# Router stage of a mixture-of-experts layer: its four batches written out and pipelined, per-chunk loads, a scan for the running counts

## The reference

```python
x = hidden_states.reshape(-1, h)
logits = jnp.einsum('th,eh->te', x, router_w)
top_vals, top_idx = jax.lax.top_k(logits, TOP_K)
top_w = jax.nn.softmax(top_vals, axis=-1)
expert = top_idx[:, 0]
weight = top_w[:, 0]
...
combine = jax.nn.one_hot(expert, e, dtype=x.dtype) * weight[:, None]
out = jnp.einsum('eth,te->th', out_e, combine)
```

```python
base = jax.nn.sigmoid(r.astype(jnp.float32)) * (num / jnp.maximum(den, 1e-08))
out = base * (0.8 + 0.2 * tf)
```

## Time and profile before

| what | value |
|---|---|
| median of 3 runs | 2638.8 us (2637.32 to 2645.15) |
| the profiled execution's own time | 2640.12 us |
| its span, first to last instruction | 2638.4 us |
| busy in the span | PE 81%, PEld 50%, DVE 67%, ACT 51%, POOL 41% |
| mean granted TensorE clock | 0.903 |

### The profile page before, as it was taken

One profiled execution on the slowest core, in us unless ns is written; L12 is line 12 of the kernel. 1 busy time (PEld: TensorE's weight loads), 2 busy tenths in 40 slices (PEclk: granted clock), 3 DMA queues, 4 the chain that ended last, 5 costly groups with the idle time before them and its releaser, 6 DMA issues. The chain is left out here.

```text
span 2638.4 us, 43862 instructions
## 1 busy us (share of the span) xinstructions
PE 2124.7 (81%) x14585; PEld 1320.6 (50%) x14585; DVE 1771.3 (67%) x3464; ACT 1349.1 (51%) x3201; POOL 1092.5 (41%) x748
## 2 busy tenths in 40 slices
PE   0688887999999999999954499727887887875899
PEld 0355554656555566666634355414555555542344
DVE  7788877888878887867643299545767677753110
ACT  4566655555555555555534133235656565635432
POOL 5656565555545565544420255443323233320000
PEclk9989998999999999999985599957888888887999
DMA  4233223211222122211125744462333232326110
GB/s 157 76 96 97 85 87 98 97 65 58 70 89 84 65 74 66 93 61 62 63 86 219 283 136 136 165 246 77 120 105 120 90 136 81 105 92 223 72 72 24
DMA packets 114027, 279.00 MB, mean 106 GB/s; under 512 B 10576, under 2 KB 40656, under 8 KB 111184
## 3 DMA queue, kind: packets, MB, share of 16 engines
q1 hardware_dynamic: 94032, 221.69, 24.8%
q10 hardware_dynamic: 17280, 46.93, 5.0%
q0 software_dynamic: 2560, 8.39, 0.8%
HBM read 188.89 MB, written 80.74 MB: 102 GB/s over the span
## 5 line engine op out<-in xcount | busy, mean ns | idle before, releaser
L828 PE MATMUL ps_q<-a_y,a_w 128*128 128x512 f16 x1536 | 355.4, 381 | 0.0
L614 POOL TENSOR_TENSOR a_rb<-a_rb,a_rot 128x512 f32<-128x512 f32 x129 | 185.9, 1441 | 308.1 <-ACT a_rb L727 308.1
L828 PEld LDWEIGHTS ps_q<-a_y,a_w 128*128 128x128 f16 x1536 | 149.3, 101 | 162.7 <-issue 4.0
L182 POOL TENSOR_TENSOR wkv_ekv<-wkv_ek,wkv_kt 128x512 f32<-128x512 f32 x66 | 100.9, 1529 | 308.6 <-DVE wkv_ek L215 308.6
L255 DVE TENSOR_TENSOR_SCAN wkv_bwd<-wk_decay,wkv_tail,wkv_fwd 128x512 f32<-128x512 f32 x130 | 215.1, 1684 | 0.7
L618 POOL TENSOR_TENSOR a_qk<-a_ra,a_rb 128x512 f32<-128x512 f32 x129 | 204.6, 1586 | 18.9 <-POOL a_rb L614 0.5
L878 PE MATMUL ps_g<-a_o,a_wo 128*128 (+1 forms) x768 | 176.3, 379 | 13.2 <-POOL a_o L605 10.6
L845 PE MATMUL ps_s<-a_qk 128*128 128x512 f32 (+3 forms) x512 | 174.1, 462 | 14.3 <-POOL a_qk L618 14.3
L837 PEld LDWEIGHTS ps_v<-a_w,a_y 128*128 128x128 f16 x3072 | 176.9, 98 | 15.1
L867 PE MATMUL ps_o<-a_tt_,a_v 128*128 128x512 f32 (+3 forms) x512 | 174.2, 487 | 11.0 <-ACT a_tt_ L745 9.4
L837 PE MATMUL ps_v<-a_w,a_y 128*128 128x128 f16 x3072 | 182.0, 219 | 0.0
(11 more groups left out here) (249 smaller groups left out, 4876.3 us busy)
## 6 DMA issues: line engine op xcount, KB each, us to landing
a_w<-wqkv_split SPq DMA_DIRECT2D x48, 768.0 KB, 4.3
scratch_numlog<-wkv_nl ACTq DMA_DIRECT2D x48, 512.0 KB, 2.8
wkv_kt<-in_fT ACTq DMA_DIRECT2D x67, 256.0 KB, 2.7
a_wraw<-in_wqkv SPq DMA_DIRECT2D x18, 768.0 KB, 5.5
wqkv_split<-a_w SPq DMA_DIRECT2D x17, 768.0 KB, 7.1
a_stacks<-qk_parts SPq DMA_DIRECT2D x102, 128.0 KB, 2.6
gate_up<-in_gate_up SPq DMA_DIRECT2D x8, 1408.0 KB, 23.5
a_nlc<-scratch_numlog SPq DMA_DIRECT2D x18, 512.0 KB, 4.1
```

The source lines that it names most:

```text
L614: pool.tensor_tensor(rb[:, n, :], rb[:, n, :], rot[:, 2 * n + 1, :], ALU.mult).then_inc(s["roped"], 1)
L828: mm = pe.matmul(psq[n][:], w16[:, i % 2, wp, n, c, :], y16[:, yp, c, :], start=c + m == 0, stop=c == CC - 1 and m == 2)
```

## The change

What it does, all of it in `moe_route`:

- The loops over the batches are written out. `mr_xt` has two buffers, y is written in place in them, and `mr_yt` is gone. Batch b uses buffer b % 2.
- SP issues x of batches 0 and 1 without a wait, x of batch b >= 2 once the transposes of batch b-2 are done (`rows_ps`). The division's terms come in four DMAs of 512 KB, one for each chunk, each of which waits for that chunk's y of the batch before. ACT's first exp waits for x alone; DVE waits for its chunk's terms.
- The copies of a batch's rows on ACT, and of its logits on DVE (with the 8 largest of its four tiles, which were all taken at the end), stand behind the next batch's elementwise work. PE has two banks for logits and four for rows.
- The 16 dependent additions become one scan over 128 columns, expert-major, with a factor of 0 where an expert's row begins (`going`, made by POOL). The counts now include the tile itself, so the constant matrix `prior` changes from 1 and 0 to 0 and -1. The memset of the first count is gone.

```diff
-        xt = sb("xt", [P, CC, T])
+        xt = sb("xt", [P, 2, CC, T])
         nl = sb("nl", [P, CC, 2, T])
-        yt = sb("yt", [P, CC, T])
...
                 for b in range(B):
-                    if b:
-                        sp.wait_ge(s["sig"], b * CC)
-                    sp.dma_start(xt[:], d["x1"][b].rearrange("c p n -> p c n")).then_inc(s["x_loaded"], 16)
-                    if b:
-                        sp.wait_ge(s["y"], b * CC)
-                    sp.dma_start(nl[:], d["numlog"][1, b].rearrange("c p m n -> p c m n")).then_inc(s["x_loaded"], 16)
+                    if b >= 2:
+                        sp.wait_ge(s["rows_ps"], (b - 1) * TT)
+                    sp.dma_start(xt[:, b % 2], d["x1"][b].rearrange("c p n -> p c n")).then_inc(x_loaded[b % 2], 16)
+                    for c in range(CC):
+                        if b:
+                            sp.wait_ge(s["y"], (b - 1) * CC + c + 1)
+                        sp.dma_start(nl[:, c], d["numlog"][1, b, c]).then_inc(nl_loaded[c], 16)
                 for e in range(E):
                     sp.dma_start(w.gate_up[:, e], d["gate_up"][:, e]).then_inc(w.loaded[e], 16)
                     sp.dma_start(w.down[:, e], d["down"][:, e]).then_inc(w.loaded[e], 16)
...
-                with act.Fori(0, B) as b:
-                    act.wait_ge(s["x_loaded"], b * 32 + 32)
+                for b in range(B):
+                    y = xt[:, b % 2]
+                    act.wait_ge(x_loaded[b % 2], b // 2 * 16 + 16)
...
-                    for t in range(TT):
-                        act.wait_ge(s["rows_ps"], b * TT + t + 1)
-                        act.activation(rows[:, bass.ds(b * TT + t, 1), :].rearrange("p a n -> p (a n)"),
-                                       pst[t % 2][:], ACT.Copy).then_inc(s["rows"], 1)
+                    if b:
+                        take_rows(b - 1)
+                take_rows(B - 1)
...
-                with pe.Fori(0, B) as b:
+                for b in range(B):
+                    y = xt[:, b % 2]
                     pe.wait_ge(s["y"], b * CC + CC)
+                    if b >= 2:
+                        pe.wait_ge(s["logits"], b - 1)
...
                     for t in range(TT):
-                        if t >= 2:
-                            pe.wait_ge(s["rows"], b * TT + t - 1)
+                        if b:
+                            pe.wait_ge(s["rows"], (b - 1) * TT + t + 1)
...
-                then(dve.memset(before[:, 0, :], 0.0))
...
-                for i in range(NT):
-                    then(dve.tensor_tensor(before[:, i + 1, :], before[:, i, :], onehot[:, i, :], ALU.add))
+                then(dve.tensor_tensor_scan(upto.rearrange("p e t -> p (e t)"), going[:].rearrange("p e t -> p (e t)"),
+                                            chosen.rearrange("p e t -> p (e t)"), 0.0, ALU.mult, ALU.add))
 
                 dve.wait_ge(s["exp"], 1)
```

More of the change, by code:

```diff
@@ L1103, in moe_route @@
         expertf = sb("expertf", [P, SLOT_TILES])
-        spare = xt[:].rearrange("p c n -> p (c n)")
+        spare = xt[:, 0].rearrange("p c n -> p (c n)")
         def after_loads(lo, n, m):
             return spare[:, lo:lo + n * m].rearrange("p (n m) -> p n m", m=m)
-        pick, onehot, place = (after_loads(i * 256, NT, E) for i in range(3))
-        before, past, over = after_loads(768, NT + 1, E), after_loads(1024, SLOT_TILES, E), after_loads(1280, E, NT)
-        psr = ctx.enter_context(nc.psum_tensor("psr_l", [P, 512], F32))
-        pst = [ctx.enter_context(nc.psum_tensor(f"psr_t{i}", [P, 512], F32)) for i in range(2)]
+        pick, place = after_loads(0, NT, E), after_loads(256, NT, E)
+        chosen, upto, over = (after_loads(i * 256, E, NT) for i in range(2, 5))
+        onehot = chosen.rearrange("p e t -> p t e")
+        past = after_loads(1280, SLOT_TILES, E)
+        psr = [ctx.enter_context(nc.psum_tensor(f"psr_l{i}", [P, 512], F32)) for i in range(2)]
+        pst = [ctx.enter_context(nc.psum_tensor(f"psr_t{i}", [P, 512], F32)) for i in range(TT)]
         pss = ctx.enter_context(nc.psum_tensor("psr_s", [P, 512], F32))
         s = {n: k.sem("mr_" + n) for n in (
-            "router", "x_loaded", "const", "sig_step", "sig", "lsum", "inv", "y", "logits_ps", "logits", "rows_ps",
+            "router", "const", "sig_step", "sig", "lsum", "inv", "y", "logits_ps", "logits", "rows_ps",
             "rows", "math", "sums", "exp", "slots", "scattered")}
+        x_loaded = [k.sem(f"mr_x_loaded{i}") for i in range(2)]
+        nl_loaded = [k.sem(f"mr_nl_loaded{c}") for c in range(CC)]
         with nc.Block() as block:
@@ L1136, in _ @@
                 pool.memset(ones[:], 1.0).then_inc(s["const"], 1)
-                pool.memset(prior[:], 1.0).then_inc(s["const"], 1)
+                pool.memset(prior[:], 0.0).then_inc(s["const"], 1)
                 pool.iota(first[:], pattern=[[-1, E]], base=E, channel_multiplier=0,
@@ L1143, in _ @@
                           allow_small_or_imprecise_dtypes=True).then_inc(s["const"], 1)
-                pool.wait_ge(s["const"], 5)
-                pool.affine_select(out=prior[:], in_=prior[:], compare_op=ALU.is_gt, fill=0.0, base=0,
+                pool.memset(going[:], 1.0).then_inc(s["const"], 1)
+                pool.wait_ge(s["const"], 6)
+                pool.memset(going[:, :, 0:1], 0.0).then_inc(s["const"], 1)
+                pool.affine_select(out=prior[:], in_=prior[:], compare_op=ALU.is_gt, fill=-1.0, base=0,
                                    pattern=[[1, P]], channel_multiplier=-1).then_inc(s["const"], 1)
@@ L1201, in _, with take_logits @@
             def _(dve):
-                with dve.Fori(0, B) as b:
+                def take_logits(b):
+                    dve.wait_ge(s["logits_ps"], b + 1)
+                    dve.tensor_copy(logits[:, b * TT:(b + 1) * TT, :],
+                                    psr[b % 2][:, 0:TT * E].rearrange("p (t e) -> p t e", t=TT)).then_inc(s["logits"], 1)
+                    dve.wait_ge(s["logits"], b + 1)
+                    for i in range(b * TT, (b + 1) * TT):
+                        m = dve.max(top[:, i, :], logits[:, i, :])
+                    return m
+                for b in range(B):
+                    y = xt[:, b % 2]
                     for c in range(CC):
                         dve.wait_ge(s["sig"], b * CC + c + 1)
-                        guarded_log(dve, yt[:, c, :], nl[:, c, 1, :], yt[:, c, :]).then_inc(s["lsum"], 1)
+                        dve.wait_ge(nl_loaded[c], b * 16 + 16)
+                        guarded_log(dve, y[:, c, :], nl[:, c, 1, :], y[:, c, :]).then_inc(s["lsum"], 1)
                     for c in range(CC):
                         dve.wait_ge(s["inv"], b * CC + c + 1)
-                        fomd = k.wkv["fomd"][:, bass.ds(b, 1), c * LAYERS + 1]
-                        conditioned(dve, yt[:, c, :], nl[:, c, 0, :], fomd, yt[:, c, :]).then_inc(s["y"], 1)
-                    dve.wait_ge(s["logits_ps"], b + 1)
-                    dve.tensor_copy(logits[:, bass.ds(b * TT, TT), :],
-                                    psr[:, 0:TT * E].rearrange("p (t e) -> p t e", t=TT)).then_inc(s["logits"], 1)
-                dve.wait_ge(s["const"], 6)
-                dve.wait_ge(s["logits"], B)
-                for i in range(NT):
-                    m = dve.max(top[:, i, :], logits[:, i, :])
+                        conditioned(dve, y[:, c, :], nl[:, c, 0, :], k.wkv["fomd"][:, b:b + 1, c * LAYERS + 1],
+                                    y[:, c, :]).then_inc(s["y"], 1)
+                    if b:
+                        take_logits(b - 1)
+                m = take_logits(B - 1)
+                dve.wait_ge(s["const"], 8)
                 step = Tally(k.sem("mr_step"))
@@ L1246, in _ @@
                 then(dve.tensor_scalar(base[:], base[:], float(P), None, ALU.mult))
-                then(dve.tensor_tensor(place, pss[:, 0:NT * E].rearrange("p (t e) -> p t e", t=NT),
+                then(dve.tensor_tensor(place, pss[:, 0:NT * E].rearrange("p (e t) -> p t e", t=NT),
                                        base[:].unsqueeze(1).to_broadcast([P, NT, E]), ALU.add))
```

24 lines of the change are left out of this document (14 added, 10 removed).

## The result

The changed kernel is faster, by less than forecast. The median of its 6 runs is 2625.84 us (2621.36 to 2629.64) against 2644.26 us (2637.32 to 2646.47) for the kernel before in 6; the ratio is 0.9938 with a 95% interval of 0.9926 to 0.9950, that is 16 us less (13 to 20), where I had 25, a ratio of 0.9905. (The two medians lie 18.4 us apart; the ratio and its interval are the better measure, since runs of either kernel spread over some 8 to 9 us.) The profiled execution has a span of 2619.6 us against 2638.4, 18.8 less.

The account below looks back on a forecast made before the run. Bound by the router stage's batch-after-batch chain and its DMA of weights and scatter, ending within about a microsecond. 2640.1 us less 24.4 (PE's earlier next-stage start) and 0.6 (clock) gives 2615.1, against the median 2614; range 2604 to 2624.

Parts of the forecast that it names:

- the weights' drain: Router stage: DMA engines stay full with x, terms, weights and scatter to 1472.8, where before it was 1492.4.
- tail and scan: Router stage after the last logits: 2.1 us saved, but worth nothing by themselves under 8 us of slack.
- the new wait for ACT's exp: DVE behind the scan: could arrive at 9.6 us after the logits' start, waits to 11.6 for ACT's exp.
- the stage ends at 1460.7 + 4.6 = 1465.3: Router stage's end: scatter issued by 1460.7, next stage's first loads 4.6 us later, 30.4 us earlier than before.
- a landing that queues behind the weights: Next stage's first loads: 0.6 to 2.5 us behind the weights, about 1 to land; PE starts at 1475.0.
- The queue that holds the slot tiles back: SP's queue keeps order, so slot tiles issued at 1465.3 land behind the weights, after 1472.8; PE starts 24.4 us earlier.
- the first rival: Next stage's start: slot tiles aren't held, the chain's end decides; 30.4 us, 2608, or 2603 with higher clock; chance 0.15.
- Batch 2's y: Router stage: x issued at 1400.1, landed at 1405.6, y complete at 1413.5, after PE idles 2.8 us.
- The clock's term: PE in batch 1, partly at 2.4 GHz: x of batch 3 through earlier, up to 1.5 us, taken as 0.6.
- The second rival: Router stage's loads of terms: pieces don't overlap, 16.4 us a batch in place of 8.0; about 14 us, 2625; chance 0.13.
- the third: Written-out loops' instruction loads wait under full DMA engines: nothing gained (2639) or slower (2669); chance 0.03 for one, 0.03 for two.

Follow-up runs that it names:

- e10: Changed kernel with each expert's weights issued in 7 DMAs of shorter rows in place of 2; 2623.8 us in one run.
- e2: Changed kernel with the scan taken back to 16 dependent small operations on DVE; 2625.0 us in one run.
- e6: Changed kernel with a batch's terms in one DMA again, in place of four; 2629.4 us in one run.
- e7: Changed kernel with two of eight experts' weights issued in the next stage, behind its third slot tile's load; 2614.7 us, ratio 0.9904 to the kernel before.
- e12: Changed kernel with expert 0's weights issued ahead of batch 2's x load, where the DMA engines were idle; 2620.9 us, ratio 0.9914 to the kernel before.
- e4: Changed kernel with three of eight experts' weights issued in the next stage, ahead of its third slot tile's load; 2622.02 us, ratio 0.9928 to the kernel before.
- e8: Changed kernel with three experts' weights in the next stage, behind its third slot tile's load, and four buffers of x; 2608.9 us, ratio 0.9878.
- e1: Changed kernel with all expert weights issued in the next stage, behind its first two slot tiles; 2645.73 us in one run.

## Why the prediction was right and wrong

From the stage's start, forecast and measured:

| step | forecast | measured |
|---|---|---|
| ACT's first exp | 5.9 | 6.1 |
| PE takes batch 2 | 37.8 | 40.4 |
| weights issued | 38.2 | 40.7 |
| first scatter | 64.9 | 66.9 |
| DMA engines drained | 97.1 | 97.6 |
| next stage begins | 89.6 | 100.6 |
| PE works in the next stage | 99.3 | 104.2 |

**Right:** what bounds it. The chain is 28 us shorter and the weights' drain under 20 us earlier, so the drain decides, tail and scan are worth nothing by themselves, and the new wait for ACT's exp is 1.7 us. The drain was met to 0.5 us, and that in part by luck: the weights were issued 2.5 us late, and from their issue to the drain it was 56.9 us where I had 58.9.

**Wrong:** the step "the stage ends at 1460.7 + 4.6 = 1465.3". I took it that the scatter, once issued, lands beside the weights as before, because it had 44.9% of the engines and that is nearly what POOL can issue. That was the mean over a stretch in which the weights ran out; beside them it has 32%. So the stage's end is itself held by the weights, and what I put behind the drain was too short: not a landing that queues behind the weights (1.6 to 3.5 us), but the scatter's last landing and the barrier (3.0 us, the last 1.8 of them behind the landing) and then a whole fresh load of the slot tiles (3.6 us), 6.6 where I had 2.2. That is 4.4 of the 4.9 us by which PE's start missed; the drain's 0.5 is the rest. The sign of the mistake could have been read: in the kernel before, too, the next stage came 3.3 us behind the drain, and PE 3.7 us behind that the earlier trace rows. With these two on the forecast drain PE starts at 1472.8 + 3.3 + 3.7 = 1479.8, 19.6 us earlier; 19.5 were measured. The sum took 0.6 us more for the clock, 25.0 in all, and so missed the stage by 5.5.

The queue that holds the slot tiles back exists, as e10 shows (10.8 us to landing), but in the changed kernel nothing is queued any more when they are issued. My test for it, "If PE's first work follows the issue by under 5 us, the held queue is wrong and the first rival right", was met (3.6 us) and yet the first rival, 2608, was wrong as well: I had not thought of a third case, in which the scatter holds the stage open until the weights are through.

**Small terms.** Batch 2's y came 2.5 us later than forecast: y of batch 0 came 0.7 late, x of batch 2 landed in 6.7 us and not in 5.5, and DVE then waited 0.6 us for the last of its terms. Why this x took 6.7 us stays open: four loads of terms were issued right behind it, but so they were in batch 0, where x took 5.6, and in batch 2 of e2, where it took 5.5. In return PE had its higher clock in batch 1, and x of batch 3 was issued 32.0 us after the stage's start and not at 35.0, so that it had landed before the weights were issued and less was left to move. That made up for the late weights in the drain. The clock's term, 0.6 us, was meant for this.

The second rival (pieces that don't overlap) and the third (loading of instructions) found nothing: e6 is slower, not faster, and the written-out loops run without gaps beside full DMA engines. The range of 2604 to 2624 was too narrow at its upper end for the step that failed, and the median lies 1.8 us above it. That it lies outside is also the baseline's doing: I worked from a median of 2638.8 us in 3 runs, and in 6 runs it is 2644.3. The measured ratio on 2638.8 would give 2622.4. The miss that counts is the 25 us that I forecast against the 16 (13 to 20) measured.

## What to carry to other kernels

When a chain and a bulk prefetch end at the same time, shorten neither alone: hold back the part of the prefetch that isn't needed first, or issue it into the DMA engines' idle time, and look at what the end of the stage waits for (e7, e12). Read a queue's share in stretches in which both queues have work, not in one in which one of them runs out. And a load that is moved must not stand behind a wait on its issuer that others need to pass (e4, e8).

## What the runs showed of the hardware

- Beside 7.2 KB packets of one queue, 3.3 KB packets of another got 32 to 33% of the DMA engines (406 packets beside 400 in 10 us); beside 2.2 KB packets they got 50%, all they asked for. The Trainium skill (DMA: Bandwidth & Descriptors, Queues, rings and completion order) says that an engine alternates between queues packet by packet. The traces agree: also from 1465 to 1470 it was 171 packets beside 176, now of 9.0 KB, and the scatter's share was 28.0%. I should have worked out the share from it.
- A scatter's last piece with nothing beside it landed 2.7 us after its issue (e1), and the next stage's first load went out 1.8 us behind that landing; beside the weights it landed after 12.7 us, and the 1.8 stayed.
- In the changed kernel PE's granted clock rose from its lower level, 1.2 GHz, to its higher one, 2.4 GHz, when PE had worked on batches 0 and 1 for 10.1 us without a gap (0.51 in the microsecond from 1402, 1.00 from 1403), and the 32 small matmuls then took 3.80 us and not 6.97. In which batch it was granted the higher level differed between runs of nearly the same program (batch 1 in the changed kernel, batch 3 in e2, both in e12, neither in e10).
